# Counting stage: the high one-hot with the slot index innermost, read by TensorE at a step of eight

## What is computed

```
h = relu(layernorm(x))                                  # layer 0: attention, softmax over edges of one source
hW = h @ W;  alpha = leaky_relu(s_src[row] + s_dst[col])
ex = exp(alpha - m[row]);  denom = segment_sum(ex, row) + (E - deg) * exp(-m)
x = x + segment_sum((ex / denom[row]) * hW[col], col) + bias
h = relu(layernorm(x))                                  # layer 1: an MLP on each edge
msg = relu([h[row], h[col], edge_attr] @ W1 + b1) @ W2 + b2
x = x + segment_sum(msg, row)
```

## Time and profile before

| | |
|---|---|
| median of 3 runs | 6182.07 us |
| profiled execution | 6198.27 us, its span 6196.5 us |
| counting loop: first to last transpose (L362) | 67.9 to 377.0 us |
| loads of L353, first to last | 68.4 to 381.7 us |
| VectorE busy in the loop: L340, L341 | 136.5 us, 119.5 us |
| VectorE waited for TensorE's matmuls of the loop | 79.5 us |
| ScalarE waited for TensorE's matmuls / for prefix stores | 98.2 us / 77.3 us |

### The profile page before, as it was taken

One profiled execution on the slowest core, in us unless ns is written; L12 is line 12 of the kernel. 1 busy time (PEld: TensorE's weight loads), 2 busy tenths in 40 slices (PEclk: granted clock), 3 DMA queues, 4 the chain that ended last, 5 costly groups with the idle time before them and its releaser, 6 DMA issues. The chain is left out here.

```text
span 6196.5 us, 110907 instructions
## 1 busy us (share of the span) xinstructions
PE 4449.7 (72%) x23829; PEld 3487.0 (56%) x23830; DVE 4123.9 (67%) x7504; ACT 1599.3 (26%) x3277; POOL 3349.7 (54%) x3489
## 2 busy tenths in 40 slices
PE   3656777777777777500299976788888888888886
PEld 3545655666666666400288862566666666666665
DVE  7754555555555555418999976677777777777774
ACT  2421111111111111000166652233333333333332
POOL 1247777777777777500000000677777777777772
PEclk9987888888888888755699988999999999999998
DMA  9834555555555554690000022554555555555556
GB/s 268 307 87 116 131 130 130 135 128 129 135 132 134 131 135 132 89 62 0 0 0 0 0 62 63 151 142 137 140 139 138 139 137 140 137 140 137 140 135 96
DMA packets 1028467, 725.53 MB, mean 117 GB/s; under 512 B 763322, under 2 KB 846068, under 8 KB 1028316
## 3 DMA queue, kind: packets, MB, share of 16 engines
q1 hardware_dynamic: 685932, 391.40, 28.5%
q0 software_dynamic: 131616, 276.04, 15.7%
q10 hardware_dynamic: 210896, 57.82, 3.9%
HBM read 563.05 MB, written 161.88 MB: 117 GB/s over the span
## 5 line engine op out<-in xcount | busy, mean ns | idle before, releaser
L1061 POOL DMA_INDIRECT g_q<-q_d,g_rec x1664 | 1655.6, 995 | 1873.1 <-DMA g_lrow<-low_row_d 1342.4
L561 POOL DMA_INDIRECT rec_d<-rec,place x1568 | 1566.7, 999 | 554.6 <-issue 499.6
L1178 PE MATMUL g_hp<-pw,g_mix 128*128 x3328 | 938.3, 404 | 289.2 <-DVE g_q L1087 247.6
L1098 DVE TENSOR_TENSOR agg<-agg,g_ap 128x256 f32 x1664 | 697.7, 419 | 581.6 <-PE g_ap L1189 444.8
L655 PE MATMUL lk<-tab_sd,low 128*128 128x196 f32 x3136 | 1066.0, 428 | 0.0
L1178 PEld LDWEIGHTS g_hp<-pw,g_mix 128*128 128x128 f32 x3328 | 566.0, 189 | 659.8 <-issue 615.7
L1142 ACT ACTIVATE g_hid<-g_q 128x512 f32<-128x512 f32 x832 | 523.8, 630 | 1517.9 <-DVE g_q L1087 1132.9
L1189 PE MATMUL g_ap<-g_hid,g_oh 128*128 128x256 f32 x3328 | 877.1, 386 | 42.0 <-DVE agg L1098 27.1
L602 DVE TENSOR_REDUCE rank<-equal 128x4 f32<-128x512 bf16 x392 | 253.6, 681 | 919.1 <-ACT equal L543 918.6
L543 ACT ACTIVATE equal<-rk,minus_two 128x512 bf16<-128x512 f32 x392 | 251.4, 684 | 1946.1 <-DMA rec_d<-rec,place 873.3
L1189 PEld LDWEIGHTS g_ap<-g_hid,g_oh 128*128 128x128 f32 x3328 | 599.9, 190 | 190.9 <-issue 119.4
(11 more groups left out here) (222 smaller groups left out, 4499.0 us busy)
## 6 DMA issues: line engine op xcount, KB each, us to landing
low_row<-rows_d SPq DMA_DIRECT2D x392, 256.0 KB
rec_d<-pad SPq DMA_DIRECT2D x64, 936.0 KB, 5.6
g_rec<-rec_d SPq DMA_DIRECT2D x208, 288.0 KB
rec<-in_ea ACTq DMA_DIRECT2D x196, 256.0 KB
hx_row<-rows_d SPq DMA_DIRECT2D x392, 98.0 KB
g_lrow<-low_row_d SPq DMA_DIRECT2D x208, 128.0 KB
g_q<-q_d,g_rec POOLq DMA_INDIRECT x1664
rec_d<-rec,place POOLq DMA_INDIRECT x1568
```

The lines of the kernel that those rows point to most:

```text
L561: pool.indirect_dma_start(rec_d, bass.IndirectOffsetOnAxis(ap=place[0:n, par, j:j + 1], axis=0), rec[0:n, par, j, :], None).then_inc(s_sc[ ...
L1061: pool.indirect_dma_start(qg[:, par, j, :], None, q_d, bass.IndirectOffsetOnAxis(ap=rec[:, par, j, F_IDX:F_IDX + 1].bitcast(I32), axis=0)) ...
L1098: v.tensor_tensor(to, to, ap[j // 2 % 2][:, j % 2 * HID:(j % 2 + 1) * HID], ALU.add).then_inc(s_agg, 1)
L1178: mm = pe.matmul(hp[u][:, k * HID:(k + 1) * HID], mix[:, par, 2 * u + k, :], pw[:, bass.ds(b[k], 1), :].rearrange("p o f -> p (o f)"), sta ...
```

## The change

The high one-hot's buffer is turned from [slot, high value] to [high value, slot], as the low one-hot's already is. VectorE compares the eight high digits of the partition, repeated over the 49 values, with the first 49 rows of `iota_g`, where it compared each digit, repeated 49 times, with `iota_b`. TensorE reads slot j's 49 columns at a step of eight elements, where they were neighbours. The number, shape and order of the instructions on every engine and their waits are the same.

```diff
--- before.py
+++ after.py
@@ -177,7 +177,7 @@
                 from_dst = sb("from_dst", [P, 2], F32, ctx)
                 pick = sb("pick", [P, NB], F32, ctx)
                 oh_low = sb("oh_low", [P, 2, P, G], BF16, ctx)
-                oh_high = sb("oh_high", [P, 2, G, NB], BF16, ctx)
+                oh_high = sb("oh_high", [P, 2, NB, G], BF16, ctx)
                 pre = sb("pre", [P, FOUR, G * NB], F16, ctx)
                 hist = [pb(f"hist{k}", ctx) for k in range(2)]
                 tp, mp = pb("l0_tp", ctx), pb("l0_mp", ctx)
@@ -338,8 +338,8 @@
                         freed(v, s_hist, g)
                         tile = lambda a: a[:, bass.ds(g, 1), :].rearrange("p o j -> p (o j)")
                         v.tensor_tensor(oh_low[:, par, :, :], row(tile(low_src), P, P, G), iota_g[:, :, :], ALU.is_equal)
-                        v.tensor_tensor(oh_high[:, par, :, :], col(tile(high_src), P, G, NB), row(iota_b[:, 0:NB], P, G, NB),
-                                        ALU.is_equal).then_inc(s_oh, 1)
+                        v.tensor_tensor(oh_high[:, par, :, :], row(tile(high_src), P, NB, G), iota_g[:, 0:NB, :], ALU.is_equal
+                                        ).then_inc(s_oh, 1)
 
                     pairs(v, onehot, NG)
 
@@ -351,7 +351,7 @@
                             pe.wait_ge(s_pre, g - 1)
                         for j in range(G):
                             mm = pe.matmul(hist[par][:, j * NB:G * NB], oh_low[:, par, :, j],
-                                           row(oh_high[:, par, j, :], P, G - j, NB), start=(j == 0), stop=(j == G - 1),
+                                           row(oh_high[:, par, :, j], P, G - j, NB), start=(j == 0), stop=(j == G - 1),
                                            skip_group_check=True)
                         mm.then_inc(s_hist, 1)
```

## The result

The changed kernel takes 6592.71 us at the median of four runs (6589.14 to 6597.75), the kernel before 6184.53 us on the same occasion (6180.73 to 6191.53, four runs). The ratio is 1.0659, 95% interval 1.0641 to 1.0678: 408 us slower, where 81 us were forecast. The direction was right and the size was not; the time lies far above the range.

A forecast was written before the change was run, and what follows sets the result against it. The loop was taken as bound by a path through TensorE and VectorE, then by TensorE alone: 5.15 + 4 x 0.73 = 8.07 us an iteration, +81 us in all, 6263 us. The range was 6215 to 6345 us.

The forecast's parts named there:

- TensorE's path as the bound: Counting loop: TensorE is late everywhere, its own chain of 5.15 us setting the iteration once its three waits vanish.
- x: Extra TensorE time per group of 1764 columns from reading the high one-hot at a 16-byte step; taken as 0.73 us.
- 5.15 + 4x: Loop iteration: TensorE's chain without waits plus the extra time of four groups, forecast as 8.07 us.
- the doubled column: TensorE's moving read: a spaced column costs 0.412 ns more, the contiguous price once again, 0.73 us per group.
- The far bound: TensorE's stream: whole strided weight load taken as column time, 1.26 us extra per group, +184 us, 6366 us.
- DMA's share: Padded iterations: DMA asks for 6.7 us, no longer sets the pace, and covers 0.88 us of each iteration's loss.
- VectorE's build: High one-hot build on VectorE: 360 ns instead of 610, worth something only while VectorE is waited for.
- The first rival: TensorE streams spaced columns without penalty: 6174 us with the gain hidden (chance 0.10), 6158 us with gain everywhere (0.05).
- The lower clock: TensorE held at 1.2 GHz in the loop, spaced column 0.92 ns: +138 us, 6320 us; chance 0.13.
- The rule of two accesses to a line: Skill's note on SBUF: at least two accesses to a 16-byte line hide the memory's latency; a new line each time pays.
- The sum: Whole loop: 48 x 8.07 against 309.1 us is +78.3 us, last iteration 2.3 us, in all +81 us.

The follow-up runs named there:

- the fixed tile: Kernel before plus 24 matmuls of 392 columns per iteration, reading a tile of ones at eight steps; 0.93 ns a column at step 4, 1.80 at step 8.
- The two kernels that read at a step of 8: The changed kernel, 6592.71 us, and one with only TensorE's spaced read, VectorE comparing in the old order: 6594.72 us, ratio 1.0664 to the kernel before.
- the step of 4: High one-hot laid out with four slots innermost, so TensorE reads every fourth element; 7459.87 us, ratio 1.0118 to the kernel before on the same, slower chip.
- the step of 2: High one-hot laid out with two slots innermost, so TensorE reads every second element; 7402.91 us, ratio 1.0031 to the kernel before on the same, slower chip.
- pairs: Kernel before plus matmuls of 392 columns whose moving operand is pairs of neighbours every 16 bytes; 0.92 ns a column.
- the version with every digit four times: Kernel before with ScalarE writing each digit four times ahead of the loop, VectorE comparing runs of four, one-hot contiguous for TensorE; 6179.77 us, ratio 0.9988.

## Why the prediction was wrong

- **TensorE's path as the bound**: right. With the column price from the durations, 0.93 ns at a step of 4 (on the fixed tile) and 1.78 ns in the changed kernel, x is 0.91 and 2.41 us, and 5.15 + 4x gives 8.8 and 14.8 us; measured are 8.43 and 14.61, with 0.3 us of slower product and transpose in each. So the form holds, and a price from durations is some 5 to 11% too high; in the changed loop itself x was 2.28 us.
- **The size of x**: wrong, and this is the step that failed. The prediction took "the doubled column", 0.73 us, from the surplus of the loop's own weight loads, 46 ns spread over 128 columns (0.36 ns, which is 13% below 0.412 and not "within a tenth"). The price of a line is 1.8 ns, four times the contiguous column and more. The load does not show it: 128 of its columns at this step cost 62 ns where a stream of 128 pays 230. Nor is a load's duration a fixed part and 128 cycles, as the prediction had it: contiguous loads follow one another in 25 ns. The row was from the right step, by the other reader. A hint stood in the trace of before, where the last two matmuls of a group start 47 ns apart, less than the 53 ns of 128 cycles at 2.4 GHz. The far bound, 1.26 us, rested on the same row and was no bound.
- **DMA's share**: right in kind. It held the padded iterations before and does not any more; with the true x it cushions the same 0.88 us in each.
- **VectorE's build**: 397 ns against 360 taken; of no weight here, as said.
- **The first rival** (no penalty) is what the loop does when the moving read stays contiguous: 5.38 us per iteration where 5.3 was worked out, 7 us in all where 8 was. It did not apply to this change.
- **The lower clock** (the third rival, given 0.13): it came, through the whole loop, and its cost was misjudged. The spaced column is no cheaper or dearer for it: 1.8 ns at either level, where the rival had 0.92 from the load rows. What it added are 0.34 us of an iteration where 0.5 was estimated. That the loop had fewer gaps than before, which spoke against it, did not prevent it: PE was busy for 46.33 of 50 us. The two kernels that read at a step of 8 stayed at the lower level throughout; in the loop the step of 4 had 0.80, the step of 2 had 1.00 and the kernel before 0.97. What in the spaced read keeps the clock down was not tried.
- **The rule of two accesses to a line**, in the Trainium skill (SBUF — State Buffer, the note on cachelines under "Door 1: The DMA port swizzle"): half of it holds. Lines of 16 bytes are what the prices follow, and going to another line each time does cost. But two accesses to a line do not hide it, with 0.92 ns a column for pairs, and the stride of eight bf16 that the note lists as free costs 1.80.
- **The sum**: 48 x 14.61 - 309.1 = 392 us, and 9 in the last iteration, against 78 and 2 forecast. Of 14.61 us, 5.15 are the chain, 9.1 the counting and 0.34 the clock.

## What to carry to other kernels

Before laying an operand out for VectorE, ask who reads it afterwards. TensorE's moving operand wants at least four bf16 columns from each 16 bytes; if the layout can't have that, count the lines that a matmul opens, at 1.8 ns each, and compare with 0.41 ns a column. Where VectorE's faster form is wanted, repeat the small input instead of turning the output, as the version with every digit four times does. And take the price of an access from the same kind of reader: the step that a weight load bears for 62 ns costs a stream of as many columns 230. Before a clock of 1.00 is believed, hold a duration of an instruction that did not change against the same one at a recorded 1.00 and 0.50.

## What the runs showed of the hardware

- Moving operand in SBUF: 1.8 ns for every new 16-byte line, bf16 and fp32 alike, at granted clocks of 1.00 and 0.50 alike (step of 16), and 1.70 to 1.84 ns from 16 to 64 bytes.
- Each of the two instructions of an fp32 matmul: 0.82 ns a contiguous column.
- Weight loads of 128 bf16 columns: 25 ns apart contiguous, 62 ns apart at 16 and at 32 bytes.
- Granted clock: with the moving operand at a step of 16 bytes TensorE stayed at the lower level for the whole loop (67 to 783 us), though busy for over 90% of it; an fp32 transpose of 128 columns took 474 ns there, 328 at 1.00.
- VectorE comparing 392 bf16 elements: 610 ns with one input repeated innermost, 558 ns with runs of two, 399 with runs of four, 397 with runs of eight. Written at a step of 16 bytes, with the digit repeated innermost, it took 1963 ns, 5 ns an element; whether the write alone does this or TensorE's reads beside it was not tried.
